# A three-layer interaction network on one core: VectorE's split products stand in SBUF instead of PSUM, and the last layer's activation in PSUM instead of SBUF

## What is computed

```
for i, S in enumerate([128, 128, 128]):
    Wr = Ws[i].reshape(39, Fk, S)
    out = relu(einsum('bfd,bgd,fgs->bsd', x, h, Wr) + b[i])
    h, direct = (out[:, :64], out[:, 64:])     # last layer: direct = out
    outs.append(direct)
result = sum(concatenate(outs, axis=1), axis=-1)
```

## Time and profile before

| what | value |
|---|---|
| time, median of 3 runs | 618.65 us (618.04 to 619.49) |
| the profiled execution's own time | 617.64 us |
| its span, first to last instruction | 615.8 us |
| TensorE matmul busy | 565.6 us, 92% |
| VectorE busy | 533.5 us, 87% |
| GpSimd busy | 517.9 us, 84% |
| ScalarE busy | 376.3 us, 61% |
| mean granted TensorE clock | 0.969 of full speed |

### The profile page before, as it was taken

One profiled execution on the slowest core, in us unless ns is written; L12 is line 12 of the kernel. 1 busy time (PEld: TensorE's weight loads), 2 busy tenths in 40 slices (PEclk: granted clock), 3 DMA queues, 4 the chain that ended last, 5 costly groups with the idle time before them and its releaser, 6 DMA issues.

```text
span 615.8 us, 8529 instructions
## 1 busy us (share of the span) xinstructions
PE 565.6 (92%) x2032; PEld 386.3 (63%) x2032; DVE 533.5 (87%) x514; ACT 376.3 (61%) x421; POOL 517.9 (84%) x231
## 2 busy tenths in 40 slices
PE   0658368999999999999999999999999999999997
PEld 0325235666676667667676767767666766777665
DVE  2426609999999989899999999999999999999975
ACT  1423514857667576758576676757676675767653
POOL 0345556898998989898998989898989989898995
PEclk9797697999999999999999999999999999999999
DMA  8999985999999999999999999999999999986001
GB/s 207 238 217 237 224 189 141 193 238 191 231 205 206 211 210 218 175 223 189 224 212 202 217 203 230 197 226 197 220 197 222 201 197 218 204 213 151 0 2 34
DMA packets 33071, 118.74 MB, mean 193 GB/s; under 512 B 6817, under 2 KB 6945, under 8 KB 30928
## 3 DMA queue, kind: packets, MB, share of 16 engines
q1 hardware_dynamic: 33056, 118.57, 87.7%
HBM read 118.02 MB, written 0.52 MB: 192 GB/s over the span
## 4 chain that ended last, share of the span: by engine, by line
PE 80%; DMA 8%; SPq 5%; issue 3%; POOL 1%; DVE 1%; ACT 1%; POOLq 0%; DVEq 0%; ACTq 0%
PE acc L458 80%; SPq L247 4%; DMA xwide<-x 4%; DMA xshift<-x 2%; DMA xrep<-x 2%; POOL z_lo L220 1%; DVE z_raw L343 1%; SPq L236 0%; SPq L230 0%; DVE z_whole L343 0%; SPq L280 0%; ACT h L528 0%; ACT last L528 0%; DVE z_psum L343 0%; ACT z_hi L525 0%
## 5 line engine op out<-in xcount | busy, mean ns | idle before, releaser
L220 POOL TENSOR_TENSOR z_lo<-z_raw,z_hi 128x1024 fp32r<-128x1024 f32 (+2 forms) x224 | 512.0, 2325 | 82.1 <-ACT z_hi L525 81.9
L525 ACT CAST z_hi<-z_raw 128x1024 fp32r<-128x1024 f32 (+2 forms) x224 | 225.8, 1018 | 154.2 <-DVE z_raw L343 137.4
L343 DVE TENSOR_TENSOR z_raw<-h,xwide 128x1024 f32<-128x1024 f32 x192 | 230.9, 1218 | 27.1 <-DMA xwide<-x 13.4
L458 PE MATMUL acc<-z_hi,w_hi 128*128 128x512 f32 (+2 forms) x560 | 224.2, 470 | 12.9 <-ACT z_hi L525 6.6
L458 PE MATMUL acc<-z_hi,w_lo 128*128 128x512 f32 (+2 forms) x560 | 184.1, 398 | 0.0
L458 PE MATMUL acc<-z_lo,w_hi 128*128 128x512 f32 (+1 forms) x528 | 172.7, 401 | 9.8 <-POOL z_lo L220 5.2
L458 PEld LDWEIGHTS acc<-z_hi,w_hi 128*128 128x128 f32 (+2 forms) x560 | 106.6, 191 | 76.1 <-issue 47.9
L458 PEld LDWEIGHTS acc<-z_hi,w_lo 128*128 128x128 f32 (+2 forms) x560 | 106.4, 190 | 28.8 <-issue 3.8
L458 PEld LDWEIGHTS acc<-z_lo,w_hi 128*128 128x128 f32 (+1 forms) x528 | 99.0, 189 | 38.9 <-POOL z_lo L220 10.6
L458 PE MATMUL acc<-z_whole,w_whole 128*128 128x512 f32 x256 | 121.5, 597 | 0.0
L458 PE MATMUL acc<-z_whole,w 117*128 117x512 f32 x128 | 65.6, 637 | 24.2 <-DVE z_whole L343 24.2
(11 more groups left out here) (16 smaller groups left out, 90.3 us busy)
## 6 DMA issues: line engine op xcount, KB each, us to landing
xwide<-x SPq DMA_DIRECT2D x320, 256.0 KB, 13.5
xshift<-x SPq DMA_DIRECT2D x45, 546.0 KB
xrep<-x SPq DMA_DIRECT2D x48, 78.0 KB
xwide<-w SPq DMA_DIRECT2D x2, 1024.0 KB, 23.2
xshift<-x SPq DMA_DIRECT2D x3, 312.0 KB
xshift<-x SPq DMA_DIRECT2D x3, 234.0 KB
w_whole<-w_rest SPq DMA_DIRECT2D x1, 512.0 KB, 18.3
w<-w0a SPq DMA_DIRECT2D x1, 409.5 KB
```

The costliest lines, as they stand in the source:

```text
L220: return eng.tensor_tensor(lo[0:rows, 0:n, :], z[0:rows, 0:n, :], hi[0:rows, 0:n, :].bitcast(F32), ALU.subtract)
L343: nc.vector.tensor_tensor(dst, in0, in1, ALU.mult).then_inc(made[kind], 1)
L458: return nc.tensor.matmul(dst, w[0:rows, PLACE[layer, t], :], z[0:rows, t - G * g, :], start=first and t == 0, stop=final and t == TILES[l ...
L525: nc.scalar.copy(z_hi[0:rows, slot("PV", pair, par, pos, HI_RING), 0:n, :], src).then_inc(hi_made, 1)
```

## The change

The tile `z_psum` (PSUM) is replaced by `z_v` (SBUF) of the same shape; all that wrote or read it does so at the new place: VectorE's product of a V group, ScalarE's rounding of it, and VectorE's subtractions. The tile `last` moves from SBUF to PSUM. No instruction is added, removed or moved, and no semaphore wait differs.

```
-        last = sb("last", [128, N])
+        last = psum("last", [128, N])
-        z_psum = psum("z_psum", [128, G, N])
+        z_v = sb("z_v", [128, G, N])
@@ products
-                    dst = z_psum[0:rows, 0:n, :]
+                    dst = z_v[0:rows, 0:n, :]
@@ subtract
-                take(nc.vector, z_psum,
+                take(nc.vector, z_v,
                      z_hi[:, slot("PV", pair, par, pos, HI_RING)],
                      z_lo[:, slot("PV", pair, par, pos, LO_RING)], layer, g).then_inc(lo_made["V"], 1)
@@ high_part
-                    src = z_psum[0:rows, 0:n, :]
+                    src = z_v[0:rows, 0:n, :]
```

## The result

The changed kernel takes 696.3 us (median of 4 runs, 692.18 to 697.76) against 618.35 us before (4 runs): a ratio of 1.1247, 95% interval 1.1209 to 1.1285. It is slower by 78 us; 698 was forecast.

A forecast was written before the change was run, and what follows sets the result against it. TensorE was taken as the bound at 34.25 us a step; VectorE's 33.1 + 5.8 + 0.5 = 39.4 us would replace it, 5.15 more over 15.5 steps, 80 us, giving 698 us; range 645 to 748 (8 in 10).

The forecast's parts named there:

- The bound: Steady stretch: TensorE, never idle at 34.25 us a step, gives way to VectorE, whose slack is 1.17 us a step.
- The deciding term: VectorE's six subtractions a step each wait out GpSimd instructions: 5.8 us of waits plus 0.5, step 39.4 us; chance 0.46.
- lost overlap: VectorE's subtractions no longer overlap the neighbouring instruction: (1.22 - 1.13) x 6, another 0.5 us a step.
- 37.0 to 42.7: Ends of the step under exclusion, in us: one engine at a time holding the path, up to full waits with pairs split.
- The pair split: Lines 217 and 218: GpSimd always takes its turn between the pair; 42.7 us a step, 750 us; chance 0.20.
- The step count: 64 V groups, 4 a step, two hidden in the start-up: 15.5 steps x 5.15 = 80 us.
- TensorE's idle time: TensorE waits behind VectorE's delayed products, idling 5 us a step in pieces of about 1 to 2 us.
- The small terms: Own costs of moved operands: rounding 32 ns longer, `relu2` 33 ns shorter, `sum_last` zero; together under 0.3 us a step.
- The new form alone: VectorE's 1024-column subtraction with two SBUF inputs, without interference: 1226 ns against 1216, less than 0.1 us a step more.
- 65 ns gain: Skill page's estimate per VectorE subtraction: 58 fixed cycles from SBUF against 120 from PSUM, some 65 ns shorter.
- TensorE's clock: Risk that TensorE, left idle in pieces, is granted less clock; no loss taken at 34.25 busy of 39.4 us.
- Sharing without exclusion: Rival: VectorE and GpSimd overlap but run slower, neither blocking; 680 us at twice the time, 640 at half more; chance 0.22.

The follow-up runs named there:

- V_LAG runs: The changed kernel with V_LAG = 3 or 1 in place of 2, each VectorE subtraction one product later or earlier in its queue: 689.77 us and 709.63 us.
- pairs_in_sbuf: Against the kernel before, with WHOLE_RING = 3: z_v in SBUF only for V groups that end a layer (lines 217 and 218); 668.8 us, ratio 1.0788.

## Why the prediction was right

- **The bound** moved as said: from TensorE to VectorE, which is busy 431.0 of 432.0 us.
- **The deciding term**, six waits of 1.2 x 0.81 us and 0.5 of lost overlap, 6.3 us a step, measured 6.1 (39.18 - 33.08). Its parts were less well founded than its sum. The waits alone are 6.3 us in the step shown (six durations of 11.50 us together, less 5.20 of their own), not 5.8. The lost overlap isn't there: the subtraction of 372.70 ends at 375.91 and the next product starts at 375.83, 0.08 us before that, where the overlap was 0.09 in the kernel before (337.26 + 1.22 against 338.39). These two errors cancel. (The busy time grew by a little less than the waits, in part because the products took 1214 ns in place of 1218, by their means.) Nor are the waits spread evenly; they are locked to a pattern, 2.0, 0.2, 1.9, 2.1, 0.2 and 0 us. That six such arrivals came near the mean is luck: the V_LAG runs, for which the same sum would have given about the same, show what other patterns give, 38.3 and 40.6 us a step, both inside 37.0 to 42.7.
- **The pair split** was made a rival of its own, and it happens in one pair of two, so that its 42.7 us a step did not come: line 218 waits 2.1 us for a GpSimd instruction that got between in the first pair, and not at all in the second, where GpSimd had nothing to do. The second pair falls where GpSimd was waiting for ScalarE before the change, too.
- **The step count**: 5.02 x 15.5 = 77.8 of the 80.2 us between the spans. The rest is not assigned.
- **TensorE's idle time** was forecast at 5 us a step and is 2.5, because its matmuls also took longer: busy 404.2 / 11 = 36.7 us a step in place of 34.25. It didn't matter to the time, since VectorE sets the step.
- **The small terms**: ScalarE's rounding rose from 1017 to 1050 ns (32 forecast), `relu2` fell by 27 ns (33 forecast), `sum_last` rose by 5 (0 forecast). The new form alone takes 1216 ns, not 1226: those 10 ns aren't there. The 65 ns gain estimated from the Trainium skill ("VectorE: DVE Perf Modes", section on the TRN2 errata) isn't there either.
- **TensorE's clock** fell to 0.96 in the steady stretch, where no loss was taken. VectorE is busy 431.0 of the 432.0 us there and TensorE idle for 28, so it did not reach the end.
- **Sharing without exclusion**, the likeliest of the rivals, is out: an unhindered subtraction keeps its own time, and a held one takes its own time after the other has ended. The Trainium skill ("SBUF — State Buffer", section "Who interferes with whom") has it that the second to start blocks fully and that a GpSimd instruction that only writes doesn't count; the encounters above agree on both, with 1.08 us left after GpSimd's end at 372.70 and 0.92 us for the MEMSET at 112.23. They agree less well on who is second: at 372.33 of pairs_in_sbuf VectorE was waiting already when GpSimd's instruction of 374.36 began, and that one went first.

## What to carry to other kernels

Where VectorE and GpSimd work side by side, look at the inputs of VectorE's two-tensor instructions before moving a tile: one input in PSUM lets them overlap, two in SBUF make each wait for whole GpSimd instructions that read SBUF. As a first estimate, price it as a wait of half a GpSimd instruction per VectorE instruction (1.2 us here; 1.05 was measured), set against VectorE's slack per step, and expect the true figure to depend on the moments at which the two meet. In this kernel the instructions of 0.7 us paid as much as the one of 1.2 us (0.94 and 1.03 us against 0.96), so count such instructions, not their columns.

## What was not expected of the hardware

A waiting VectorE instruction can lose its turn twice: 5.05 us for a work of 0.68, with two GpSimd instructions ahead of it, in every second step of the kernel with only the pairs in SBUF. So one GpSimd instruction, 2405 ns, which the prediction took for the most that a wait can cost, is not the most. In the steps between, and in the changed kernel, a similar arrival had its turn after one. What decides between the two when both wait was not settled, and GpSimd's recorded ends are too rough to read it from differences of 0.1 us.
